# One weight matrix read through casting DMAs at each use instead of through a bf16 copy made once, and twice as many casts in the first phase

## What is computed

```python
xn = layernorm(x)
# attention, 16 heads; keys and values from a convolution of stride 2
q = xn @ q_w.T + q_b
xd = depthwise_conv(xn, conv_w, stride=2) + conv_b
k, v = xd @ k_w.T + k_b, xd @ v_w.T + v_b
attn = softmax(q k^T / 8) v            # 2048 queries, 1024 keys
a = attn @ out_w.T + out_b
# FFN, one expert per token
e = argmax(xn @ W_router)
h = gelu(xn @ W1[e] + b1[e])           # computed for all 4, then selected
f = layernorm2(h @ Wo + bo + xn)
out = x + a + f
```

## Time and profile before

| | |
|---|---|
| timed runs | 4892.01 us median of 2 (4888.98 to 4895.03) |
| the profiled execution | 4890.6 us, span of its slowest core (core 2) 4889.1 us |
| spans of the eight cores | 4861.9 to 4889.1 us |
| mean granted TensorE clock of the cores | 0.863 to 0.867 |
| busy on the slowest core | PE 3769.3 us (77%), DVE 1969.6 (40%), ACT 1605.7 (33%), POOL 182.7 (4%) |
| memory read, written | 486.81 MB, 58.72 MB |

### The profile page before, as it was taken

One profiled execution on the slowest core, in us unless ns is written; L12 is line 12 of the kernel. 1 busy time (PEld: TensorE's weight loads), 2 busy tenths in 40 slices (PEclk: granted clock), 3 DMA queues, 4 the chain that ended last, 5 costly groups with the idle time before them and its releaser, 6 DMA issues.

```text
span 4889.1 us, 53687 instructions; the slowest of 8 cores (4861.9 to 4889.1 us)
## 1 busy us (share of the span) xinstructions
PE 3769.3 (77%) x15040; PEld 1494.9 (31%) x15040; DVE 1969.6 (40%) x3364; ACT 1605.7 (33%) x2501; POOL 182.7 (4%) x341
## 2 busy tenths in 40 slices
PE   4477999504998888898834479999699899889883
PEld 3331122101343333343313331222233334334331
DVE  1222467401323625525541214577233352452554
ACT  3321466301322323313304323466132232331330
POOL 1011111110000000000000000000000000000000
PEclk9996599856999999999965586699799899999997
DMA  5255444443324432433321110000133433333332
GB/s 119 62 100 103 89 84 83 86 88 98 127 112 159 155 147 112 160 119 144 124 81 49 35 35 18 1 1 1 63 129 120 161 140 145 136 144 124 155 117 86
DMA packets 97347, 490.26 MB, mean 100 GB/s; under 512 B 12000, under 2 KB 12032, under 8 KB 55088
## 3 DMA queue, kind: packets, MB, share of 16 engines
q1 hardware_dynamic: 59680, 385.93, 21.0%
q0 software_dynamic: 37392, 100.89, 11.6%
HBM read 486.81 MB, written 58.72 MB: 112 GB/s over the span
## 4 chain that ended last, share of the span: by engine, by line
PE 56%; DMA 26%; issue 7%; DVE 5%; ACT 4%; SPq 0%; DVEq 0%; POOL 0%; ACTq 0%; POOLq 0%
PE ps L945 29%; DMA castslot<-w 10%; DMA w1r<-scrW 9%; PE ps L1009 9%; PE psOT L577 3%; PE psS L669 3%; DMA castslot<-wo 3%; PE psC L464 2%; PE psA_r L361 2%; PE psA_tr L341 2%; PE psBC L600 1%; PE psOT L630 1%; DMA rowsl<-rows 1%; ACT arena L287 1%; ACT arena L291 1%
## 5 line engine op out<-in xcount | busy, mean ns | idle before, releaser
L945 PE MATMUL ps<-xnT,w1r 128*128 128x512 bf16 x8192 | 1849.1, 386 | 230.0 <-DMA w1r<-scrW 177.5
L945 PEld LDWEIGHTS ps<-xnT,w1r 128*128 128x128 bf16 x8192 | 796.6, 99 | 1279.7 <-issue 389.3
L954 ACT ACTIVATE gbuf<-ps,b_sb 128x512 bf16<-128x512 f32 x1024 | 701.5, 687 | 1355.3 <-PE ps L945 1096.1
L678 ACT ACTIVATE etb<-psS 128x1024 bf16<-128x1024 f32 x512 | 522.9, 1023 | 421.2 <-PE psS L669 403.2
L1009 PE MATMUL ps<-wor,interT 128*128 128x512 bf16 x2048 | 444.2, 379 | 8.5 <-ACT gbuf L954 7.9
L963 DVE TENSOR_TENSOR sel<-gbuf,mbc 128x512 bf16<-128x512 bf16 x256 | 108.8, 425 | 831.9 <-ACT gbuf L954 831.6
L577 PE MATMUL psOT<-etb,v 128*65 128x512 bf16 x1024 | 376.3, 456 | 0.0
L669 PE MATMUL psS<-qT,kT 64*128 64x512 bf16 x1024 | 367.1, 445 | 4.0 <-DVE v L522 2.0
L341 PE MATMUL psA_tr<-eye_f,arena 128*128 128x128 f32 x256 | 98.0, 445 | 328.6 <-DVE arena L326 292.6
L590 DVE RECIPROCAL arena<-psOT 1x512 f32<-1x512 f32 x64 | 214.5, 3352 | 216.2 <-PE psOT L577 215.3
L1009 PEld LDWEIGHTS ps<-wor,interT 128*128 128x128 bf16 x2048 | 199.2, 98 | 253.5 <-issue 16.2
(11 more groups left out here) (104 smaller groups left out, 2769.7 us busy)
## 6 DMA issues: line engine op xcount, KB each, us to landing
w1r<-scrW SPq DMA_DIRECT2D x256, 1024.0 KB, 7.5
wor<-scrWo SPq DMA_DIRECT2D x64, 1024.0 KB, 5.7
castslot<-w POOLq DMA_DIRECT2D x128, 256.0 KB, 5.0
scrW<-castslot POOLq DMA_DIRECT2D x128, 256.0 KB, 3.2
arena<-x SPq DMA_DIRECT2D x16, 1024.0 KB, 6.8
arena<-x SPq DMA_DIRECT2D x32, 512.0 KB, 5.5
out<-arena SPq DMA_DIRECT2D x32, 512.0 KB, 2.9
castslot<-wo POOLq DMA_DIRECT2D x32, 256.0 KB, 5.0
```

The source lines that it names most:

```text
L678: E.emit("scalar", lambda s, par_=spar, pair_=pair, eo=eoff: s.activation(etb_t[:, eo + pair_ * 1024:eo + (pair_ + 1) * 1024], ps_s[par_][ ...
L945: t_.matmul(ps8[:, gp_ * 512:(gp_ + 1) * 512], w1r[:, sl_, cc_ * 512 + ic_ * 128:cc_ * 512 + (ic_ + 1) * 128], xnT[:, cc_, 8 + tb_ * 512:8 ...
L954: E.emit("scalar", lambda s, e_=e, icg_=icg, gp_=gpar: s.activation(gbuf[:, icg_ % 2, e_, :], ps8[:, gp_ * 512:(gp_ + 1) * 512], AF.Gelu, ...
```

## The change

Wo is no longer copied to bf16 ahead: the list of casts holds W1's 128 alone. A Wo tile is loaded from the fp32 input by GpSimd, cast on its way into `wor`, at the same place in the program as before; its semaphore is `sWog`. Phase A writes six casts behind each tile pair instead of three. `scrWo` stays declared and is not used.

```diff
-    for piece in range(NE * NIS + NIS):
+    for piece in range(NE * NIS):
         for half in range(4):
             sl = half % 2
-            if piece < NE * NIS:
-                srcap = w1_d[piece, :, half * 1024:(half + 1) * 1024]
-                dstap = scrW1[piece, :, half * 1024:(half + 1) * 1024]
-            else:
-                srcap = wo_d[piece - NE * NIS, :, half * 1024:(half + 1) * 1024]
-                dstap = scrWo[piece - NE * NIS, :, half * 1024:(half + 1) * 1024]
+            srcap = w1_d[piece, :, half * 1024:(half + 1) * 1024]
+            dstap = scrW1[piece, :, half * 1024:(half + 1) * 1024]
             cast_state["ops"].append((piece, sl, srcap, dstap))
...
             if b == 0:
-                drain_cast(3)
+                drain_cast(6)
...
         def emit_wo_load(tb, is_):
             slot = is_ % 2
-            w = [(sT, m_wosl.get(slot, 0))] + list(m_scr[NE * NIS + is_])
-            E.emit("sync", lambda s, p_=is_, sl_=slot: s.dma_start(
-                wor[:, sl_, :], scrWo[p_, :, :]),
-                waits=w, incs=[(sWo[slot], 16)])
-            m_wold[(tb, is_)] = (sWo[slot], sWo[slot].n)
+            w = [(sT, m_wosl.get(slot, 0))]
+            E.emit("gpsimd", lambda g, p_=is_, sl_=slot: g.dma_start(
+                wor[:, sl_, :], wo_d[p_, :, :]),
+                waits=w, incs=[(sWog[slot], 16)])
+            m_wold[(tb, is_)] = (sWog[slot], sWog[slot].n)
```

## The result

The change makes the kernel slightly slower, by less than 1%: the ratio of its time to that of the kernel before is 1.0063, 95% interval 1.0038 to 1.0088, that is some 31 us on 4890. The forecast was 4843, 1% faster. The profiled execution took 4902.5 us, with a span of 4900.9 against 4889.1 before; the timed ones lay from 4911 up, so the profile shows the smaller part of the difference, 12 us. Some executions, among them the profiled one of `e5_pool_plain_d6`, had one die at a lower clock; they are left out of every ratio here, and that profile is read on a core of the other die.

A forecast was written before the change was run, and what follows sets the result against it. POOL's one-time bf16 weight casts, with Wo's as the whole gap before batch 0's FFN, were taken to bound the kernel. From 4890.6 us, -105 (earlier FFN), +47 (Wo stalls) and +10 (rowsl waits) gave 4843 us; range 4792 to 4921.

The forecast's parts named there:

- What bounds the kernel: Before batch 0's FFN: POOL's weight casts sit on the critical path; Wo's 32 are the whole gap, some 190 us.
- Part 2: Phase A, six casts per tile pair: Q load 85 us late, at 323; FFN starts at 1042, gaining 105 (79 to 115).
- Part 3: Second FFN matmul stage: Wo cast loads land in 8.0 us, too late for tiles 2, 4 and 6; cost 47 us.
- 24 stalls x 2.0 = 47 us: Second FFN matmul stage: tiles 2, 4 and 6 each 2.0 us late in all 8 stages, 47 us together.
- the bound of 99: Second FFN matmul stages, upper bound if loads can't overlap and pass at one in 9.0 us: 99 us over 8.
- The sign that was to warn of this: Wo loads in the second FFN matmul stage: a landing over 10 or under 6.2 us would show that term wrong.
- Part 4: SP's queue: earlier W1 loads bring no gain; rowsl loads at both FFN starts cost 5 us each, 10 us together.
- The sum: Whole kernel: -105 + 47 + 10 = -48 against 4890.6 us, giving 4843; own range 4797 to 4921.
- (a): Rival, second FFN matmul stage: Wo cast loads hide wholly; 4776 to 4796 us in all; chance 12%.
- (b): Rival, second FFN matmul stage: under eight cores' load each Wo load lands after 12.2 us, costing 148; 4944 us; chance 19%.
- (c): Rival, second FFN matmul stage: W1 prefetch and casts delay each other, landing 17.20 us, costing 268; 5064 us; chance 7%.

The follow-up runs named there:

- e5_pool_plain_d6: The changed kernel with Wo tiles loaded by POOL as plain bf16 from the copy of W1, without the use of Wo: 0.9823 of the kernel before.
- e2_cast_d3: The changed kernel with three casts per tile pair in phase A instead of six: 0.9871 of the kernel before, span 4820.6 us.
- e6_fill: The changed kernel with 13 additional zero-weight matmuls behind tiles 1, 3 and 5 of the second matmul stage: 0.9978 of the kernel before, span 4898.6 us.
- e1_sp_plain_d6: The changed kernel with SP loading plain bf16 pieces of W1 in place of Wo's cast loads: 0.9795 of the kernel before, span 4785.7 us.
- three-slot kernel: The changed kernel with four casts per tile pair and Wo tiles 2 and 5 in GELU's buffer: 0.9699 of the kernel before, span 4739.5 us.

## Why the prediction was wrong

**What bounds the kernel: right.** The Wo casts were the gap in front of batch 0's FFN, and without them the gap closed from 210 to 29 us. The memory read was 537.15 MB, as worked out (537).

**Part 2: right.** The Q load went out at 324.9 us (323 said, 313 to 349 as bounds) with no idle time before it, attention ended at 1028.9 (1022 said; as a mean over the cores it ends 88 us later than before, where 85 was said). `e2_cast_d3` shows the delay to be the additional casts'. The gain to the FFN's start was 89.6 instead of 100.

**Part 3: the kind of wait right, its size wrong by half.** This is the step that failed: "24 stalls x 2.0 = 47 us". The stages grew by 92.7 us, inside the bound of 99, but the value taken from between the bounds was too low, and more than half of what was missed came from a mechanism that the forecast did not have. Two terms:

- The waits came to 65.8 us, in 34 pieces. Tiles 2, 4 and 6 alone waited in four stages, 3.1 us each time in the mean; in the other four the lateness was spread over more tiles. The best loads landed in 7.8 to 8.1 us, the 8.0 of the forecast; but the median was 8.7 and the late ones took 9 to 10.3 (the two early ones of each batch, which nothing waits for, up to 24.7). The forecast's own formula gives 24 x (8.7 + 0.9 - 6.94) = 64 us with the median in it. I had worked a time from quiet rows and used it for all. The sign that was to warn of this, a landing over 10, did not come: the median lies inside the 7 to 9 that was said, where 0.7 us more make 17 us in the sum.
- The granted clock. The 2048 matmuls took 27.6 us more in busy time, of which the forecast had nothing. `e6_fill` removed all but 3.8 of it by giving PE something to do in the waits. Behind the three waits of the first stage it cost PE a further 1.7, 2.8 and 1.7 us (15.66 and 16.81 against 13.97). The trace before had rows that would have told, and I did not look for them: its timeline of PE has 24 matmuls of L945 in 5.34 us behind a short wait, and the first 11 in 4.80 behind one of 8 us, in a window with a granted clock of 0.81.

```profile
1543.15 5.34 PE L945 MATMUL ps<-xnT,w1r 128*128 128x512 bf16 x24 [0.58 <-DMA w1r<-scrW]
...
1575.51 4.80 PE L945 MATMUL ps<-xnT,w1r 128*128 128x512 bf16 x11 [8.05 <-DMA w1r<-scrW]
```

```profile
1560.00:1576.00 16.00, 7.95 (x37) 3.43 (x36) 9.93 (x18) 3.44 (x5) 0.00 (x0) 0.81 0.47 172
```

**Part 4: right in sign, short in size.** +8.6 and +7.0 us at the two FFN starts, where I had 5 each as the most. W1's tiles moving earlier cost nothing in the stage (`e1_sp_plain_d6`), as said.

**The sum.** -48 was said; the profile has +12, the timed runs +31. With a gain of 100 and a cost of 47, a cost twice as high turned the sign. That the cost was bounded by 21 and 99 and the gain by 79 and 115 was in the text; the single number in the middle looked firmer than it was. The rivals: (a) falls, the loads do not hide; (b) has the right direction, but its landing of 12.2 was 8.7 by the median; (c) falls, tiles 4 and 6 waited like tile 2, and with no help from the W1 prefetch. Plain loads through POOL's queue landed in 5.1 us and through SP's in 4.9, and at the two FFN starts the casts of POOL's queue made the wait for SP's `rowsl` loads 8.6 and 7.0 us longer. That agrees with the rule of the Trainium skill (DMA: Bandwidth & Descriptors, section "Issuing engines are not separate DMA queues") that was weighed there. By the fit in the Trainium skill (same page, the section on the anatomy of one SWDGE DMA: 2.0 us plus bytes at 436 GB/s) a tile would have landed in 6.8 us, an estimate. None of the 64 took less than 7.8.

Not settled: what delays a load from 8 to 10 us. The core's own transfers are not enough: on the slowest core the load of tile 4 in the second stage, issued at 1722.41, had no other beside it (1.07 MB moved in all from 1722 to 1732, 1.05 of them its own) and landed in 9.2 us, the one at 1764.57 in 7.8. That in the three-slot kernel one core of each pair of neighbours waits much more than the other speaks for something that the two share. The Trainium skill (DMA: Bandwidth & Descriptors, section Bandwidth) says that two cores of a pair which both stream share their memory's bandwidth at about 358 GB/s each. A quiet cast lands at 197 GB/s and reads twice that, 394, so there would be less than it wants. No run here separates the cores, so this stays a guess. Also open is why the timed executions of the change lie 10 to 40 us above its profiled one.

## What to carry to other kernels

A transfer that is hidden by 1.2 us in every one of 64 places is not a free one: before making it longer, multiply the lateness by the places, and take the late landings, not the quiet ones. On a matmul stage at full clock add the clock's loss behind the wait to the wait itself (27.6 us to 65.8 here). And ask of every edit in the same change whether it is worth anything without its partner: here the edit that helps while the casts are last (more casts early) costs 80 us as soon as they are not. Four casts for each pair instead of six, and a third slot in a buffer that happens to be idle, turn the change from 0.6% slower into 3% faster.

## What was not expected of the hardware

- Waits of 2.3 to 4.0 us between stretches of dense matmuls were often enough to lower the granted clock, to an average of 0.91 over a stage. Their length alone does not tell: behind one of 2.28 us (at 1713.23) 64 matmuls took 15.73 us, behind one of 2.30 (at 4450.86) 13.97, and behind one of 2.83 (at 1731.79) 32 took 7.07, both at full speed. 13 matmuls with only 8 weight columns each, in the place of the wait, kept it up (mean 379 ns again).
- The same plain 1 MB load landed in 5.1 us (median) through POOL's queue and in 4.9 through SP's (core 2 of `e5_pool_plain_d6` and of `e1_sp_plain_d6`), while a cast that lands as many bytes took 7.6 us at least, in any run.
- In the three-slot kernel the sums of the stages split by core within each pair of neighbours, 442 to 443 us on one and 460 to 471 on the other.
